# GpSimd's products split by batch and interrupted, one product and the style scales given to VectorE

## The reference, cut to what matters

```python
# stage 1: a finite-difference step over 8 fields of 128 x 128
Af = A_grid[None] * f[:, None];  Bf = B_grid[None] * f[:, None]
df = -(grad(Af[:, 0], 1) + grad(Af[:, 1], 2)) \
     + 0.5 * (grad2(Bf[:, 0], 1) + grad2(Bf[:, 1], 2) + 2 mixed grads of Bf[:, 2])
x = maximum(f + df * dt[:, None, None], 0)
# stage 2: layernorm over features, then over tokens, conditioned by a small network
h = (x - mean) * rsqrt(var + 1e-5) * ln_g + ln_b
h_norm = (h - h.mean(1)) * rsqrt(h.var(1) + 1e-8)
gamma, beta = split(small_network(subj_emb[ids]))
h = h_norm * (softplus(gamma) + 1e-8) + beta
# stage 3: 8 experts of 128 -> 512 -> 128, the best 2 weighted, and a residual
y = sum_e gate_e * (relu(h @ w1[e] + b1[e]) @ w2[e] + b2[e]);  out = x + y
```

## Time and profile before

| what | value |
|---|---|
| runs | 118.77, 119.10, 119.17 us (median 119.1) |
| profiled execution: its own time | 119.23 us |
| profiled execution: its span | 117.4 us |
| PE busy | 110.7 us (94%), 512 matmuls |
| DVE busy | 91.3 us (78%) |
| ACT busy | 78.5 us (67%) |
| POOL busy | 9.9 us (8%) |
| DMA | 10.79 MB; 9.93 MB of them in queue q1 |

### The profile page before, as it was taken

How to read it: one execution, slowest core, us unless ns; L and a number is a source line. 1 busy time by engine, 2 the same in 40 slices (tenths; PEclk the granted TensorE clock), 3 DMA queues, 4 the chain that set the end, 5 groups by cost and what they waited for, 6 DMA issues and landing times.

```text
span 117.4 us, 1552 instructions
## 1 busy us (share of the span) xinstructions
PE 110.7 (94%) x512; PEld 86.3 (74%) x512; DVE 91.3 (78%) x199; ACT 78.5 (67%) x110; POOL 9.9 (8%) x20
## 2 busy tenths in 40 slices
PE   6999969999999999999999999999999999999960
PEld 2699757447646788888888888888888888888850
DVE  1475989788992596999949966996799589889781
ACT  0843446785452997777777777777777777777800
POOL 3325930000000000000000000000000000000040
PEclk9999999999999999999999999999999999999999
DMA  2999991000000370040400130040005000400005
GB/s 84 299 395 416 409 395 38 0 0 3 0 0 8 95 265 6 22 156 0 179 0 0 50 131 6 0 144 35 0 0 179 0 0 0 184 0 0 0 0 179
DMA packets 4439, 10.79 MB, mean 92 GB/s; under 512 B 784, under 2 KB 1744, under 8 KB 4432
## 3 DMA queue, kind: packets, MB, share of 16 engines
q1 hardware_dynamic: 3920, 9.93, 23.2%
q10 hardware_dynamic: 512, 0.78, 2.2%
HBM read 10.15 MB, written 0.56 MB: 91 GB/s over the span
## 4 chain that ended last, share of the span: by engine, by line
PE 89%; DVE 6%; ACT 1%; issue 1%; DVEq 0%; ACTq 0%
PE zt L701 11%; PE zt L703 11%; PE zt L702 11%; PE yt L695 6%; PE aux L726 6%; PE aux L729 6%; PE aux L725 6%; PE yt L729 5%; PE yt L726 5%; PE yt L725 5%; PE zt L677 4%; PE zt L561 3%; PE zt L688 2%; PE yt L669 1%; PE yt L584 1%; DVE vs L886 1%
## 5 line engine op out<-in xcount | busy, mean ns | idle before, releaser
L531 ACT ACTIVATE hid_hi<-zt,pv 128x1024 fp32r<-128x1024 f32 x27 | 30.2, 1118 | 17.4 <-PE zt L703 17.2
L1031 DVE TENSOR_TENSOR hid_lo<-hid,hid_hi 128x1024 fp32r<-128x1024 f32 x27 | 33.0, 1220 | 10.0 <-issue 5.4
L536 ACT ACTIVATE hid<-zt,pv 128x1024 f32<-128x1024 f32 x27 | 29.9, 1108 | 0.0
L701 PE MATMUL zt<-h_hi,ws 128*128 128x512 f32 x56 | 22.7, 406 | 0.0
L703 PE MATMUL zt<-h_lo,ws 128*128 128x512 f32 x56 | 21.8, 390 | 0.0
L702 PE MATMUL zt<-h_hi,ws 128*128 128x512 f32 x56 | 21.8, 389 | 0.0
L701 PEld LDWEIGHTS zt<-h_hi,ws 128*128 128x128 f32 x56 | 10.5, 188 | 2.9 <-issue 0.5
L702 PEld LDWEIGHTS zt<-h_hi,ws 128*128 128x128 f32 x56 | 10.5, 188 | 2.5 <-issue 0.5
L703 PEld LDWEIGHTS zt<-h_lo,ws 128*128 128x128 f32 x56 | 10.5, 188 | 2.2
L726 PE MATMUL aux<-hid_hi,ws 128*128 128x512 f32 (+1 forms) x32 | 12.0, 376 | 0.0
L725 PE MATMUL aux<-hid_hi,ws 128*128 128x512 f32 (+1 forms) x32 | 12.0, 376 | 0.0
(11 more groups left out here) (150 smaller groups left out, 149.6 us busy)
## 6 DMA issues: line engine op xcount, KB each, us to landing
we<-in_exp_w_dram SPq DMA_DIRECT2D x8, 512.0 KB, 9.1
gate_all<-gates_dram SPq DMA_DIRECT2D x8, 512.0 KB, 3.6
f<-in_x_dram SPq DMA_DIRECT2D x2, 256.0 KB, 4.6
ft<-in_x_exchanged_dram ACTq DMA_DIRECT2D x2, 256.0 KB, 5.4
out_dram<-acc SPq DMA_DIRECT2D x1, 256.0 KB, 2.1
out_dram<-acc SPq DMA_DIRECT2D x2, 128.0 KB, 2.0
first<-d_difference_dt_ids_dram ACTq DMA_DIRECT2D x1, 136.0 KB, 3.7
gn<-in_grids_dram SPq DMA_DIRECT2D x1, 128.0 KB, 3.8
```

The lines of the kernel that those rows point to most:

```text
L531: act.activation(hid_hi[:, c, :], zt[c % 2][:], ACT.Relu, bias=bias).then_inc(hi_ready, 1)
L536: act.activation(hid[:, c, :], zt[c % 2][:], ACT.Relu, bias=bias).then_inc(hid_ready, 1)
L701: pe.matmul(zt[c % 2][:, tok], w_hi, h_hi[:, tok], start=True, stop=False)
L1031: v.tensor_tensor(hid_lo[:, c, :], hid[:, c, :], hid_hi[:, c, :].bitcast(F32), ALU.subtract).then_inc(lo_ready, 1)
```

## The change

- `WARM_START` goes from 8 to 7, and `unchanged(1)` is moved ahead of `step_cross(0, ...)`.
- VectorE makes the second half's `u_a1`, right after `s_b2`.
- GpSimd starts when `u_a1` is done. It makes its three products one batch (128 x 128) at a time: four for `u_a0`, two for `u_b1`; then it waits for `gamma_ready`, and makes two more for `u_b1` and four for `u_b0`. TensorE waits for the batches that it needs.
- VectorE, not GpSimd, makes `gsum` (with the 1e-8 in it) and `gamma_g`, in two instructions after `normalise(0)`; `half_gamma` is gone, and its factor 0.5 moves into `minus_quarter_g`. VectorE waits for its own `gamma_ready`.
- ScalarE makes `glog` ahead of `normalise(0)` instead of after it; `beta` stays after it.
- The second half's first layer-1 matmul is one of 512 columns instead of two of 256, and waits for all of `h`.

```diff
-WARM_START = 8
+WARM_START = 7
@@ GpSimd
-            def product(out_, in_, grid):
-                return pool.tensor_tensor(out_[:, batches(1), :], in_[:, batches(1), :], over_batches(grid), ALU.mult)
-            pool.wait_ge(s_ready[1], 1)
+            def products(out_, in_, grid, first_batch, count, done):
+                for b in range(first_batch, first_batch + count):
+                    pool.tensor_tensor(out_[:, b, :], in_[:, b, :], grid, ALU.mult).then_inc(done, 1)
+            pool.wait_ge(a1_ready[1], 1)
+            pool.wait_ge(f_in[1], 16)
+            pool.wait_ge(gn_in, 16)
+            products(u_a0, f, a0_grid, BH, BH, a0_ready[1])
             pool.wait_ge(ft_in[1], 16)
             pool.wait_ge(gt_in, 16)
-            product(u_a1, ft, a1_grid).then_inc(a1_ready[1], 1)
-            pool.wait_ge(f_in[1], 16)
-            pool.wait_ge(gn_in, 16)
-            product(u_a0, f, a0_grid).then_inc(a0_ready[1], 1)
-            product(u_b1, ft, b1_grid).then_inc(b1_ready[1], 1)
-            product(u_b0, f, b0_grid).then_inc(b0_ready[1], 1)
-            pool.wait_ge(glog_ready, 1)
-            step(pool.tensor_tensor(gsum[:], gpos[:], glog[:], ALU.add))
-            pool.wait_ge(p128_in, 16)
-            ins = pool.tensor_scalar(half_gamma[:], gsum[:], 1e-8, 0.5, ALU.add, ALU.mult)
-            ins.then_inc(gamma_ready, 1)
+            products(u_b1, ft, b1_grid, BH, 2, b1_ready[1])
             pool.wait_ge(gamma_ready, 1)
-            pool.tensor_scalar(gamma_g[:], half_gamma[:], ln_g, 0.5, ALU.mult, ALU.mult).then_inc(gamma_ready, 1)
+            products(u_b1, ft, b1_grid, BH + 2, 2, b1_ready[1])
+            products(u_b0, f, b0_grid, BH, BH, b0_ready[1])
@@ ScalarE
             style_parts()
+            style_log()
             normalise(0)
-            style_log()
+            style_shift()
@@ TensorE, second_rows_a and second_rows_b (and second_columns_b, one batch at a time)
-                pe.wait_ge(a0_ready[1], 1)
                 for k in range(2):
                     b = BH + 2 * k
+                    pe.wait_ge(a0_ready[1], 2 * k + 2)
@@ TensorE, the order
             keep_warm(WARM_START)
             unchanged(0)
+            unchanged(1)
             pe.wait_ge(first_in, 16)
             step_cross(0, 0)
             step_cross(0, 1)
-            unchanged(1)
...
             logits(0)
-            layer1_0_first(1)
+            pe.wait_ge(h_ready, sum(H_DVE))
+            pe.wait_ge(h_act_ready, B - sum(H_DVE))
+            layer1_0(1, 0)
@@ VectorE
+            def gammas():
+                v.wait_ge(glog_ready, 1)
+                v.wait_ge(net_sb, 5)
+                then(v.scalar_tensor_tensor(gsum[:], gpos[:], 1e-8, glog[:], ALU.add, ALU.add))
+                v.tensor_scalar(gamma_g[:], gsum[:], ln_g, 0.25, ALU.mult, ALU.mult).then_inc(gamma_ready, 1)
...
-                v.wait_ge(gamma_ready, 2)
-                moved = mark(v.scalar_tensor_tensor(tg[:, hb], mh[:, hb], ln_b, half_gamma[:, hb], ALU.subtract, ALU.mult))
+                moved = mark(v.scalar_tensor_tensor(tg[:, hb], mh[:, hb], ln_b, gsum[:, hb], ALU.subtract, ALU.mult))
...
             product(s_b2, f, 1, b2_grid).then_inc(s_ready[1], 1)
+            v.wait_ge(ft_in[1], 16)
+            product(u_a1, ft, 1, a1_grid).then_inc(a1_ready[1], 1)
             feature_stats(0)
             cross_operand(1)
             normalise(0)
+            gammas()
+            v.wait_ge(gamma_ready, 1)
```

More of the change, by code:

```diff
@@ L127, in build @@
         vs2 = sb("vs2", [P, B])
-        minus_half_g = sb("minus_half_g", [P, 1])
+        minus_quarter_g = sb("minus_quarter_g", [P, 1])
         tg = sb("tg", [P, B])
@@ L154, in build @@
         gsum = sb("gsum", [P, B])
-        half_gamma = sb("half_gamma", [P, B])
         gamma_g = sb("gamma_g", [P, B])
@@ L421, in style_log, with style_shift @@
                 act.activation(glog[:], gexp[:], ACT.Ln, bias=one[:, 0:1]).then_inc(glog_ready, 1)
+            def style_shift():
                 act.activation(beta[:], small[:, B:2 * B], ACT.Identity, bias=pv[:, STY_BB:STY_BB + 1]).then_inc(net_sb, 1)
@@ L632, in second_columns_b @@
             def second_columns_b():
-                pe.wait_ge(b1_ready[1], 1)
                 for b in range(BH, B):
+                    pe.wait_ge(b1_ready[1], b - BH + 1)
                     pe.matmul(own(b), u_b1[:, b, :], half_diff2, start=False, stop=False, skip_group_check=True)
             def second_rows_b():
-                pe.wait_ge(b0_ready[1], 1)
                 for k in range(2):
                     b = BH + 2 * k
+                    pe.wait_ge(b0_ready[1], 2 * k + 2)
                     pe.matmul(pair_of(1, k), half_diff2, u_b0[:, b:b + 2, :].rearrange("p b j -> p (b j)"), start=False,
@@ L677, in layer1_0, with layer1_0_first @@
                 pe.matmul(z0[c], we[:, 0, 0, c, :], h[:, half(n)], start=True, stop=True).then_inc(z0_ready, 1)
[L679 to L683, removed]
+            def layer1_0_first():
+                h_of = h[:, half(0)].rearrange("p (k u j) -> p u k j", k=2, u=2)
                 z_of = z0[0].rearrange("p (k u j) -> p u k j", k=2, u=2)
                 for u in range(2):
-                    pe.wait_ge(h_ready, 2 * n + u + 1)
-                    pe.wait_ge(h_act_ready, 2 * n + u + 1)
+                    pe.wait_ge(h_ready, u + 1)
+                    pe.wait_ge(h_act_ready, u + 1)
                     last = pe.matmul(z_of[:, u], we[:, 0, 0, 0, :], h_of[:, u], start=True, stop=True,
@@ L794, in _ @@
             pe.wait_ge(w_in[0], 16)
-            layer1_0_first(0)
+            layer1_0_first()
             pe.wait_ge(acc_ready, 1)
@@ L909, in token_centre @@
                 shifted = mark(v.tensor_scalar(ve2[:, hb], mv2[:, hb, 1], gsq[:, 0:1], 1e-8, ALU.mult, ALU.add))
-                then(v.tensor_scalar(mh[:, hb], mv2[:, hb, 0], minus_half_g[:, 0:1], ln_b, ALU.mult, ALU.add))
-                v.wait_ge(gamma_ready, 2)
-                moved = mark(v.scalar_tensor_tensor(tg[:, hb], mh[:, hb], ln_b, half_gamma[:, hb], ALU.subtract, ALU.mult))
+                then(v.tensor_scalar(mh[:, hb], mv2[:, hb, 0], minus_quarter_g[:, 0:1], ln_b, ALU.mult, ALU.add))
+                moved = mark(v.scalar_tensor_tensor(tg[:, hb], mh[:, hb], ln_b, gsum[:, hb], ALU.subtract, ALU.mult))
                 return shifted, moved
@@ L998, in _ @@
             v.tensor_scalar(gsq[:], ln_g, ln_g, 0.25, ALU.mult, ALU.mult).then_inc(gsq_ready, 1)
-            v.tensor_scalar(minus_half_g[:], ln_g, -0.5, None, ALU.mult).then_inc(gsq_ready, 1)
+            v.tensor_scalar(minus_quarter_g[:], ln_g, -0.25, None, ALU.mult).then_inc(gsq_ready, 1)
             v.wait_ge(f_in[1], 16)
             product(s_b2, f, 1, b2_grid).then_inc(s_ready[1], 1)
+            v.wait_ge(ft_in[1], 16)
+            product(u_a1, ft, 1, a1_grid).then_inc(a1_ready[1], 1)
             feature_stats(0)
```

## The result

The changed kernel took 120.09 us as a median of 10 runs (119.48 to 121.03), the kernel before 119.18. The ratio is 1.0094, with a 95% interval from 1.0064 to 1.0124: 0.9% slower, where 1.0% faster was forecast and the range ended at 118.7. The profiled execution took 119.90 us, its span is 118.1 us.

The account below looks back on a forecast made before the run. It took TensorE to bound the kernel from the first matmul on h, VectorE and ScalarE before that. −1.15 − 0.22 + 0.35 − 0.10 = −1.12 us from a profiled 119.23 gave 118.11, as a median 118.0; range 117.4 to 118.7.

Parts of the forecast that it names:

- the start at 19.93: First matmul on h in the old profile, in us; from there the chain of waits stays on TensorE.
- My slower rival: GpSimd batches of 0.60 us or more delay xn and h: 119.6 us, chance 0.05.
- the second burst: GpSimd's last six one-batch products hold VectorE's small instructions between xn and h: cost 0.35 us, bounds 0.2 to 0.45.
- the merge: Second half's first layer-1 matmul, 512 columns instead of two of 256: 0.86 instead of 0.96 us, −0.10.
- The stall in `normalise(0)`: VectorE, held by a GpSimd product in the first half, is freed: sq to xn 0.59 instead of 1.74 us, −1.15.
- rival 6: VectorE's L886 wasn't held by GpSimd; the stall stays and only 0.3 us is gained: 118.8, chance 0.04.
- rival 3: The tensor_scalar instructions of token_centre are held by GpSimd's second burst as well: −0.92, 118.2 us, chance 0.08.
- A batch on GpSimd: One 128 x 128 product on GpSimd takes 0.45 us, with a step of 0.415 between products.
- rivals 1, 4 and 5: 1: second burst free, 117.6, chance 0.15; 4: batch 0.54, 119.0, 0.04; 5: batch 0.60 or more, 119.6, 0.05.
- `u_a1`, `glog` and the `gamma`s at 0: Work moved or reordered on VectorE and ScalarE fits into waits ahead of statistics, xn and token_stats: cost 0.
- The warm-up: One warm-up matmul less on TensorE starts real work 0.45 us earlier at half pace: −0.22, bounds 0 and 0.45.
- Rival 2: The warm-up swap gives nothing because TensorE's pace rises later: −0.90, 118.2 us, chance 0.12.

Follow-up runs that it names:

- e1: The changed kernel with an unused tile of 32 bytes per partition where half_gamma stood, restoring the old addresses: 118.79 us, ratio 0.9953.
- e2: The kernel before with half_gamma allocated last, so the tiles behind it lie 32 bytes lower, same instructions: 121.63 us, ratio 1.0217.
- f10: e1 with hid allocated behind hid_lo and 32 more unused bytes ahead of it: 118.68 us, ratio 0.9947.
- h1: e1 with GpSimd resuming its products at norm1_ready instead of waiting for gamma_ready: 118.40 us, ratio 0.9932.
- theory G: Tested by the kernel before with five more zero matmuls in TensorE's idle 1.35 us, claiming that gap makes its clock fall in some executions: 119.52 us.
- f2: The changed kernel with 32 unused bytes ahead of ws and 32 behind it: 120.13 us, ratio 1.0053.
- f8: e1 with the unused tile of 40 floats instead of 8, a shift of 128 bytes: 120.07 us, ratio 1.0030.
- f9: e1 with the unused tile of 72 floats instead of 8, a shift of 256 bytes: 118.90 us, ratio 0.9929.
- g1: e1 without GpSimd's wait for gamma_ready between its two bursts, twelve one-batch products in a row: 119.57 us, ratio 1.0034.

## Why the prediction was wrong

**The step that failed** stands in the first part: "What brings the start at 19.93 forward is therefore worth its full amount at the end, as long as nothing with a fixed time of its own comes in between", and with it "the rest of the span as before". I looked for fixed times and waits, and took the 81 us behind them, with the same instructions, to last the same. They lasted 1.64 us longer: 0.97 ahead became 0.67 behind in the spans (118.1 against 117.4). The cause is shown both ways: e1 takes it out of the changed kernel, e2 puts it into the one before. It is the removal of `half_gamma`, whose effect on the other tiles' addresses the prediction put at nothing without a reason; none of my rivals held it. My slower rival, at 119.6, was another mechanism, and it did not occur.

**The terms.** With the old addresses (e1) the profiled execution took 118.11 us, the sum to the hundredth. That is luck. It is the second shortest of e1's ten, whose mean of 118.71 is only 0.56 below the 119.27 of the kernel before on that chip (executions at 0.99 or more), half of the 1.12. And in its trace the parts differ from the sum: VectorE's first statistics began 0.48 earlier than before, not 0.22; `sq` to `xn` gave back 0.99 (0.75 instead of 1.74), not 1.15; the second burst cost 0.38, not 0.35; the merge gave nothing, not 0.10. The terms are read below from the changed kernel, where this stage took 12.47 us (from the first difference matmul on `u_a0` to the first matmul on `h`), as in f10 with the old addresses.

- The stall in `normalise(0)`, −1.15: measured, `sq` to `xn` 0.58 instead of 1.74, −1.16. Right here, and rival 6 falls. But it hangs on the first burst ending in time, which it does not in every execution (see below).
- The second burst, +0.35: `xn` to `h` 4.33 instead of 3.96, +0.37. The size was right, the place was not: `mh` (0.50 instead of 0.28) and `tg` (0.37 instead of 0.22) were held, `sq` was not. So rival 3's mechanism was the real one, at my forecast's price. The Trainium skill, "SBUF — State Buffer", section "Who interferes with whom", says that a `tensor_scalar` can take the shared ports in its two-port modes. The trace agrees in that such instructions were held: `mh`, and in h1 `gamma_g` (0.38 instead of 0.23) and `xn` (0.74 instead of 0.60).
- A batch on GpSimd, 0.45 by interpolation between 8 and 512 elements: four in 1.70 and a step of 0.415. Right; rivals 1, 4 and 5 fall.
- `u_a1`, `glog` and the `gamma`s at 0: `u_a1` ended 1.05 us before the statistics, `token_stats` started 1.12 after `xn`, where it was 1.09. Right in this profile, to 0.03.
- The warm-up, −0.22: not a property of the edit. The difference matmuls on `u_a0` started at 6.67, 6.79, 6.33 and 6.25 us in the four profiles with 8 warm-ups (mean 6.51), and between 6.11 and 7.16 in the twelve with 7 (mean 6.57). The start varies by a microsecond from execution to execution, and one matmul more or less is lost in that. Rival 2 is the nearer one.
- The merged matmul, −0.10: 0.96 either way. I took 0.86 from matmuls of another line and never asked whether this one would run at their pace.
- Not in the sum: TensorE's idle 1.35 us, with which, if theory G holds, the kernel before pays 1.6 us in about a quarter of its executions. The prediction saw the gap only as an echo.

**The cover of `u_a1`.** The prediction read from one profile that the operand had landed. VectorE's first instruction on `gt` starts between 6.69 and 8.70 us in the sixteen profiles, each time released by that transfer. In four of the twelve profiles with the pause (e1, f2, f8, f9) VectorE was late against TensorE, and `sq` to `xn` took 0.75 to 0.87: GpSimd, which waits for `u_a1`, was still at its first burst. In f2, f8 and f9 the statistics began right behind `u_a1`, without idle time. In f9 `u_a1` starts 1.74 us later than in the changed kernel, and GpSimd's first burst ends at 14.58, as `vs` does (14.60):

```profile
11.28 0.68 DVE L850 TENSOR_TENSOR u_a<-ft,gt 128x512 f32<-128x512 f32 x1
...
14.22 0.38 DVE L884 SCALAR_TENSOR_TENSOR vs<-mv,sq 128x4 f32<-128x4 f32 x1
```

```profile
13.71 0.87 POOL L361 TENSOR_TENSOR u_b<-ft,gt 128x128 f32<-128x128 f32 x2
```

From the first difference matmul on `u_a0` to the first matmul on `h` the kernel before took 13.26 us, the changed one 12.47, f9 13.53 and f8 13.64: the whole gain of the stage is gone there. No profile of the kernel before has `gt` as late, so what it would have lost isn't known. This is one likely reason why the medians gain less than the sum; how much of it is not shown.

What stays open: why the matching layer runs at 0.229 to 0.231 when the other does not match, why 128 bytes cost a little less than 32 and 64, and why both kernels run at 0.231 to 0.233 for the first six microseconds of the experts (the chain between 35 and 41 us) and only the matching one then drops. Distances other than 32, 64, 128 and 256 weren't tried, nor other operand types.

## What to carry to other kernels

A change that adds or drops a small tile moves every tile behind it; when a stage that was not edited changes its pace at an equal granted clock and with equal instructions, compare the addresses of its operands before anything else, and keep the layout fixed (an unused tile will do) while comparing schedules. On a kernel that TensorE bounds, a cost of 5.5 ns in each of some 300 matmuls is worth more than a microsecond won in the prologue, so a prediction there should hold a line for the pace of the long stage. To keep VectorE's chains of small instructions free of GpSimd, stopping GpSimd is what helps; cutting its instructions up without a pause leaves nearly the whole hold in place.

## What the runs showed of the hardware that I had not expected

- A stream of 128x512 fp32r matmuls, each with its own weights, steps at 0.2267 us when the weights and the moving operand lie a multiple of 256 bytes apart (0 and 256 tried), and at 0.232 to 0.234 when they lie 32, 64 or 128 bytes off that, at a granted clock of 1.00 (distances by the rounding to 32 bytes named above). A layer that matches, in turns with one that doesn't, steps at 0.229 to 0.231. TensorE's busy share doesn't show it; the median duration of one matmul does (0.389 or 0.390 against 0.392 to 0.397 us).
- With an idle stretch of 1.24 to 1.57 us on TensorE between 13 and 17 us (before, e2, g1), 27 of 98 executions had a mean granted clock of 0.978 to 0.986, and in the kernel before these took 1.6 us more; in the kernels whose profiles show 0.19 to 0.63 idle there, none of 87 did, and h1 had one of 0.567 in 11. That the gap is the cause is not shown.
- Back-to-back GpSimd products of 0.415 us hold four VectorE instructions in turn, for 0.2 to 0.3 us each; between two of them one VectorE instruction gets through.
